# DLRM tower on Trainium2: two of three holds on the gather queue moved and one taken away, four transposes moved down TensorE's order

## The chip, the cores and the metric

One Trainium2 chip, one core. The metric is device time in microseconds (us) of one execution. TensorE (PE) computes matrix products and transposes, its weight loads are shown apart as PEld; ScalarE (ACT) and VectorE (DVE) copy and compute element by element; GpSimd (POOL) issues the gathers here; SyncE (SP) issues the other loads.

## The reference

For 512 samples, 26 embedding rows of 128 numbers are looked up, one from each table. With the dense row they make 27 vectors, and all products of two different ones are features of a three-layer network:

```python
sd = jnp.einsum('bfd,bd->bf', sparse_values, dense_features)
ss = jnp.einsum('bfd,bgd->bfg', sparse_values, sparse_values)
z = jnp.concatenate([dense_features, sd, ss[:, iu, ju]], axis=1)   # pairs f < g
h = jnp.concatenate([z, r_dense_features], axis=1)
h = jnp.maximum(h @ W_top1 + b_top1, 0.0)      # 607 -> 512
h = jnp.maximum(h @ W_top2 + b_top2, 0.0)      # 512 -> 256
y = h @ W_top3                                 # 256 -> 1
```

## The kernel before, in words

The samples are four tiles of 128. Twelve of the smaller tables are looked up on TensorE, for all samples at once: a table is split into a high and a low part and both are multiplied by a one-hot matrix (`table` steps, L485; the second halves of the last two tables are the `L498` instructions). The other 14 tables are gathered by POOL: one indirect DMA fetches 128 rows of one table for one tile, 56 gathers in all, k = 14 t + n for tile t and table n. Those rows lie one sample to a partition, so TensorE transposes them (`batch` steps, L520), up to four tables at a time, and ACT or DVE copies the result from PSUM into `embT` (`PLACERS` says who: ACT for batch 3.2, DVE for 3.0, 3.1 and 3.3).

Each tile t then goes through: `dots` D (128 matmuls, L540), `copies` C.0 and C.1 (16 copies on ACT, L314, and 16 on DVE, L387, from `dots` to `pairs`), `dense` P (L556), `layer1` L (L567), `relu1` R (ACT, L366), `layer2` M (L584), `relu2` H (ACT L370, DVE L428), `layer3` Y (L591) and `result` V (DVE, L432). `dots` is one set of PSUM banks: D of a tile waits until both engines have copied all of the tile before, and until all four batches of its own tile are placed.

The order is written by hand in `STEPS`: a word is a step, B3.0 is batch 0 of tile 3, and each of PE, ACT and DVE takes its own share of the steps in this order. So a step that is moved moves on every engine that has a part in it. Batches have 4, 4, 4 and 2 tables. B3.0, B3.1 and B3.2 are all transposed into the PSUM bank `turned`, so each waits until the one before it has been placed; B3.3 goes into a bank of `dots` and waits for C2.1.

POOL has its own loop (L274) and no steps. Gathers 7 to 42 wait for a count of finished tables, the first of each batch of tiles 2 and 3 waits until its buffer's older rows have been transposed, and `HELD_BY_DOTS` names gathers that also wait for a D:

```python
if k in HELD_BY_DOTS:
    pool.wait_ge(dots_done, HELD_BY_DOTS[k])
```

Before, gather 37 waits for D0, 44 for D1 and 51 for D2. B2.2 needs gathers 36 to 39, B2.3 needs 40 and 41, B3.0 needs 42 to 45, B3.1 46 to 49, B3.2 50 to 53, B3.3 54 and 55.

Of the kernel before, what the change touches and what calls it, by code (L numbers as in the profile page):

```python
# [53 lines left out]
def dlrm_tower(nc, gather_ids, onehot_ids, spread, tables, dense_t, w_pairs, w_dense, small, w2, identity,  # L54
# [9 lines left out]
    GATHERS_AHEAD, GATHERS_PER_TABLE = 4, 3  # L64

    LATER_GATHERS = GATHERS_AHEAD + GATHERS_PER_TABLE * (N_ONEHOT + 1)
    HELD_BY_DOTS = {37: 1, 44: 2, 51: 3}
    PAUSED_TABLES = (4, 6, 8)
    WARMING = 29
    WARMING_BETWEEN = 6  # L70
# [4 lines left out]
    with ctx:  # L75
# [108 lines left out]
        def loads_of(i):  # L184
# [5 lines left out]
        STEPS = [(NAMES[w[0]], *map(int, w[1:].split("."))) for w in """  # L190
            T0 T1 B0.0 T2 T3 B0.1 T4 B0.2 T5 B0.3 T6 B1.0 T7 B1.1 T8 T9 B1.2 T10.0 B1.3 T11.0 B2.0 T10.1
            D0 C0.0 T10.2 T10.3 T10.4 A10 T11.1 T11.2 T11.3 T11.4 C0.1 P0 B2.1 A11
            D1 C1.0 B2.2 B2.3 L0.0 L0.1 R0.0 R0.1 C1.1 P1 B3.0 M0 H0
            D2 Y0 C2.0 V0 B3.1 L1.0 L1.1 R1.0 R1.1 C2.1 P2 B3.2 M1 H1 B3.3 L2.0 R2.0
            D3 Y1 C3.0 V1 L2.1 R2.1 C3.1 P3 M2 H2
            L3.0 R3.0 Y2 V2 L3.1 R3.1 M3 H3 Y3 V3""".split()]

# [60 lines left out]
        def _(pool):  # L258
# [4 lines left out]
            for t in range(TILES):  # L263
                for n in range(N_GATHERED):
# [3 lines left out]
                    if GATHERS_AHEAD + GATHERS_PER_TABLE <= k < LATER_GATHERS:  # L268
                        pool.wait_ge(table_selected, (k - GATHERS_AHEAD) // GATHERS_PER_TABLE)
                    if k in HELD_BY_DOTS:  # L270
                        pool.wait_ge(dots_done, HELD_BY_DOTS[k])
                    if t >= 2 and n % BATCH_T == 0:
# [395 lines left out]
```

## Time and profile before

| what | us |
|---|---|
| median of 3 runs (lowest, highest) | 110.64 (110.51, 111.36) |
| the profiled execution's own time | 110.51 |
| its span from first to last instruction | 108.6 |
| PE busy | 104.1 (96%) |
| DVE busy | 75.6 (70%) |
| ACT busy | 66.1 (61%) |
| POOL busy | 60.4 (56%) |

The granted TensorE clock is full (1.00) over the whole span. The profiled execution is the lowest of the three, 1.9 us longer than its span and 0.13 under the median.

### The profile page before, as it was taken

What the parts mean: (1) busy time and instruction counts of PE and PEld (TensorE: products, weight loads), DVE (VectorE), ACT (ScalarE), POOL (GpSimd) and SP (SyncE); (2) the same over time, 40 slices, a digit from 0 to 9 for tenths busy, and PEclk for the clock granted to TensorE, in tenths of its full rate; (3) what the DMA queues carried; (4) which work ended last, traced back from release to release, by engine and by line L of the source; (5) the groups of instructions that cost most, each with busy time, mean ns of one, the idle gap of its engine ahead of it and who ended that gap; (6) DMA issues with size and microseconds to landing.
All of it is one profiled execution on the core that took longest, in us unless ns stands there. A gap on an engine that the chain in (4) does not pass through costs nothing.

```text
span 108.6 us, 2787 instructions
## 1 busy us (share of the span) xinstructions
PE 104.1 (96%) x1095; PEld 92.9 (86%) x1095; DVE 75.6 (70%) x204; ACT 66.1 (61%) x134; POOL 60.4 (56%) x62
## 2 busy tenths in 40 slices
PE   6999999999999999999899989999999999998992
PEld 6865888888888888888699979999999999998991
DVE  2199999999999999999950880599339830287001
ACT  5555528978997999989450993529133671286120
POOL 7877877877777777777700577777537600000000
PEclk9999999999999999999999999999999999999999
DMA  2899999784999999821200022212201110000000
GB/s 67 220 257 219 247 217 247 178 239 74 312 306 293 281 330 290 223 62 50 48 24 9 21 51 54 56 50 54 63 9 48 48 30 0 6 0 0 0 6 1
DMA packets 5199, 12.75 MB, mean 117 GB/s; under 512 B 1833, under 2 KB 1961, under 8 KB 5186
## 3 DMA queue, kind: packets, MB, share of 16 engines
q1 hardware_dynamic: 3346, 8.83, 30.4%
q0 software_dynamic: 1792, 3.67, 13.2%
q8 instruction: 9, 0.15, 0.6%
q10 hardware_dynamic: 48, 0.07, 0.2%
q14 instruction: 4, 0.03, 0.1%
HBM read 12.56 MB, written 0.00 MB: 116 GB/s over the span
## 4 chain that ended last, share of the span: by engine, by line
PE 39%; DVE 33%; DMA 14%; issue 6%; SPq 3%; ACT 2%; DVEq 0%
DVE onehot L394 16%; PE dots L540 14%; DMA table<-tbl 14%; PE hidden L567 10%; DVE low L402 9%; DVE pairs L387 9%; PE hidden L584 2%; PE last_layers L584 2%; ACT high L330 2%; SPq L226 2%; PE turned L520 2%; PE turned L567 2%; PE hidden L556 2%; PE hidden L485 1%; PE last_layers L591 1%
## 5 line engine op out<-in xcount | busy, mean ns | idle before, releaser
L274 POOL DMA_INDIRECT rows<-tbl,gather_idx x56 | 57.5, 1027 | 25.6 <-issue 14.8
L394 DVE TENSOR_SCALAR onehot<-ids_h 125x512 fp32r<-125x512 f16 x98 | 35.9, 425 | 3.3 <-ACT ids_h L320 3.3
L387 DVE COPY pairs<-dots 31x128 f32<-31x128 f32 (+5 forms) x64 | 18.4, 287 | 18.3 <-PE dots L540 16.5
L314 ACT COPY pairs<-dots 31x128 f32<-31x128 f32 (+5 forms) x64 | 16.1, 252 | 14.8 <-PE dots L540 13.5
L485 PE MATMUL dots<-onehot,high 125*128 125x512 f32 (+1 forms) x66 | 24.8, 395 | 0.1
L485 PE MATMUL dots<-onehot,low 125*128 125x512 f32 (+1 forms) x66 | 23.8, 380 | 0.1
L330 ACT CAST high<-table 125x1024 fp32r<-125x1024 f32 (+2 forms) x13 | 13.1, 1004 | 8.8 <-DMA table<-tbl 8.7
L402 DVE TENSOR_TENSOR low<-table,high 125x512 fp32r<-125x512 f32 (+1 forms) x24 | 16.6, 691 | 0.4 <-ACT high L330 0.3
L540 PE MATMUL dots<-embT 128*64 128x54 f32 x512 | 15.8, 223 | 0.4 <-DVE pairs L387 0.4
L540 PEld LDWEIGHTS dots<-embT 128*64 128x64 f32 x512 | 15.3, 138 | 1.0 <-issue 0.6
L485 PEld LDWEIGHTS dots<-onehot,low 125*128 125x128 f32 x66 | 12.3, 188 | 2.9 <-DVE low L402 0.8
L485 PEld LDWEIGHTS dots<-onehot,high 125*128 125x128 f32 x66 | 12.3, 188 | 2.6 <-ACT high L330 0.3
L567 PE MATMUL hidden<-pairs,wp 128*128 128x128 f32 x112 | 13.5, 276 | 0.3 <-DVE pairs L387 0.3
L567 PEld LDWEIGHTS hidden<-pairs,wp 128*128 128x128 f32 x112 | 12.9, 192 | 0.5 <-ACT pairs L314 0.5
L485 PE MATMUL hidden<-onehot,high 125*128 125x512 f32 (+1 forms) x32 | 12.6, 398 | 0.0
L485 PE MATMUL hidden<-onehot,low 125*128 125x512 f32 (+1 forms) x32 | 11.7, 369 | 0.5 <-DVE low L402 0.3
L347 ACT COPY embT<-dots 128x512 f32<-128x512 f32 (+1 forms) x8 | 8.6, 1080 | 0.0
L320 ACT CAST ids_h<-dots 125x512 f16<-125x512 f32 x12 | 7.5, 628 | 0.9 <-PE dots L458 0.9
L314 ACT COPY embT<-turned 128x512 f32<-128x512 f32 x7 | 7.9, 1124 | 0.0
L366 ACT ACTIVATE h<-hidden 128x256 f32<-128x256 f32 x7 | 2.5, 382 | 8.5 <-PE hidden L567 8.5
L485 PEld LDWEIGHTS hidden<-onehot,low 125*128 125x128 f32 x32 | 6.0, 188 | 1.8 <-DVE low L402 0.9
L485 PEld LDWEIGHTS hidden<-onehot,high 125*128 125x128 f32 x32 | 6.0, 188 | 1.3 <-DVE onehot L394 0.2
(55 smaller groups left out, 108.0 us busy)
## 6 DMA issues: line engine op xcount, KB each, us to landing
table<-tbl SPq DMA_DIRECT2D x10, 448.0 KB
wp<-w_pairs SPq DMA_DIRECT2D x2, 512.0 KB, 5.4
rows<-tbl,gather_idx POOLq DMA_INDIRECT x56, 4.3
table<-tbl SPq DMA_DIRECT2D x1, 560.0 KB
table<-tbl SPq DMA_DIRECT2D x10, 52.0 KB
wd<-w_dense SPq DMA_DIRECT2D x1, 512.0 KB, 4.7
w2s<-w SPq DMA_DIRECT2D x1, 512.0 KB, 5.2
table<-tbl SPq DMA_DIRECT2D x2, 224.0 KB
```

Source lines behind the costliest of these rows:

```text
L274: pool.indirect_dma_start(out=rows[:, t % 2, n, :], out_offset=None, in_=tables[GATHERED_TABLES[n]][:, :], in_offset=bass.IndirectOffsetOn ...
L314: return nc.scalar.copy(dst, src)
L320: nc.scalar.copy(ids_h[:, i % ID_BUFFERS, :], relative[i % 2][0:ROW_PARTS, :]).then_inc(ids_relative, 1)
L330: nc.scalar.copy(high[i % STAGES][:, first:last, :], table[i % TABLE_BUFFERS][:, first:last, :]).then_inc(high_ready, 1)
L347: nc.scalar.copy(embT[:, samples, TABLE_SLOT[t]], selected[t % STAGES][:, samples]).then_inc(table_placed, 1)
L387: return nc.vector.tensor_copy(dst, src)
L394: nc.vector.tensor_scalar(onehot[i % STAGES][:, c, :], ids_h[:, i % ID_BUFFERS, :], float(c), None, ALU.is_equal).then_inc(onehot_ready, 1)
L402: nc.vector.tensor_tensor(low[i % STAGES][:, first:last, :], table[i % TABLE_BUFFERS][:, first:last, :], high[i % STAGES][:, first:last, : ...
L485: last = nc.tensor.matmul(selected[t % STAGES][:, samples], part[t % STAGES][:, c, :], onehot[t % STAGES][:, c, samples], start=(part is h ...
L540: last = nc.tensor.matmul(dots[64 * h:64 * (h + 1), g, 0:2 * SLOTS], embT[:, s:s + 2, :].rearrange("p u s -> p (u s)"), embT[:, s:s + 2, 0 ...
L567: last = nc.tensor.matmul(hidden_block(t, m), wp[:, c, cols(m)], pairs[:, t % 2, c, :], start=False, stop=(c == PAIR_CHUNKS - 1), skip_gro ...
L584: last = nc.tensor.matmul(results[m], w2s[:, c, 128 * m:128 * (m + 1)], h1[:, t % 2, c, :], start=(c == 0), stop=(c == CHUNKS1 - 1))
```

## The change

The table of holds has two entries in place of three: gather 38 waits for D0 and gather 42 for D1, no gather waits for D2. In the order of steps B3.0 moves from before M0 to after V0, where B3.1 stood; B3.1 moves to where B3.2 stood; B3.2 moves behind M1 and H1, directly ahead of B3.3.

```diff
-    HELD_BY_DOTS = {37: 1, 44: 2, 51: 3}
+    HELD_BY_DOTS = {38: 1, 42: 2}
...
-            D1 C1.0 B2.2 B2.3 L0.0 L0.1 R0.0 R0.1 C1.1 P1 B3.0 M0 H0
-            D2 Y0 C2.0 V0 B3.1 L1.0 L1.1 R1.0 R1.1 C2.1 P2 B3.2 M1 H1 B3.3 L2.0 R2.0
+            D1 C1.0 B2.2 B2.3 L0.0 L0.1 R0.0 R0.1 C1.1 P1 M0 H0
+            D2 Y0 C2.0 V0 B3.0 L1.0 L1.1 R1.0 R1.1 C2.1 P2 B3.1 M1 H1 B3.2 B3.3 L2.0 R2.0
```

On TensorE, between L0 (above the first row) and L2.0 (last row); the transposes are the L520 rows, and the two stretches around D2 and L1 that stay as they are lie between the two pieces:

```order
@@ -248,5 +248,4 @@
 L567 MATMUL hidden<-pairs,wp 128x128 x16
 L556 MATMUL hidden<-denseT,wd 128x128 x4
-L520 MATMUL turned<-ident,rows 128x128 x4
 L584 MATMUL last_layers<-h,w2s 128x128 x4
 L584 MATMUL hidden<-h,w2s 128x128 x4
@@ -259,4 +258,5 @@
 L584 MATMUL last_layers<-h,w2s 128x128 x4
 L584 MATMUL hidden<-h,w2s 128x128 x4
+L520 MATMUL turned<-ident,rows 128x128 x4
 L520 MATMUL dots<-ident,rows 128x128 x2
 L567 MATMUL hidden<-pairs,wp 128x128 x8
```

Four transposes stand one fewer ahead of D2, and one batch more behind M1, ahead of D3. The number of instructions between D1 and D3 is the same.

On DVE, the copies C1.1 and C2.1 (19x4x32 rows) with what follows them:

```order
@@ -72,5 +72,4 @@
 L387 COPY pairs<-dots 7x4x32 x2
 L387 COPY pairs<-dots 19x4x32 x2
-L387 COPY embT<-turned 128x4x128
 L428 TENSOR_SCALAR h<-hidden,smalls 128x128
 L387 COPY pairs<-dots 31x4x32
@@ -84,4 +83,5 @@
 L387 COPY pairs<-dots 7x4x32 x2
 L387 COPY pairs<-dots 19x4x32 x2
+L387 COPY embT<-turned 128x4x128
 L428 TENSOR_SCALAR h<-hidden,smalls 128x128
 L387 COPY embT<-dots 128x2x128
```

The placing of B3.0 no longer stands behind C1.1; the placing of B3.1 now stands behind C2.1 and ahead of DVE's half of H1. On ACT the placing of B3.2 and its half of H1 change places.

On POOL, of the change, gathers 36 to 46, with their waits:

```order
L274 DMA rows<-tbl,gather_idx 128x128 [waits transposed,table_selected]
L274 DMA rows<-tbl,gather_idx 128x128 [waits table_selected]
L274 DMA rows<-tbl,gather_idx 128x128 [waits dots_done,table_selected]
L274 DMA rows<-tbl,gather_idx 128x128 [waits table_selected]
L274 DMA rows<-tbl,gather_idx 128x128 [waits transposed,table_selected]
L274 DMA rows<-tbl,gather_idx 128x128 [waits table_selected]
L274 DMA rows<-tbl,gather_idx 128x128 [waits transposed,dots_done,table_selected]
L274 DMA rows<-tbl,gather_idx 128x128 x3
L274 DMA rows<-tbl,gather_idx 128x128 [waits transposed]
```

Gather 37 has lost its wait for a D, 38 and 42 have one; 42 has three waits, and behind it only the waits for free buffers are left.

## Rows read from the trace of the kernel before

**Rows 1.** The chain of waits, in order of time: start us, length us, what.

```profile
55.89 3.90 PE dots L540 x128
...
64.58 0.30 DVE pairs L387
...
65.02 3.94 PE dots L540 x128
...
73.35 0.89 PE hidden L556 x8
74.24 0.44 PE turned L520 x4
74.68 0.89 PE last_layers L584 x8
75.57 0.89 PE hidden L584 x8
76.46 3.87 PE dots L540 x128
...
90.38 3.90 PE dots L540 x128
94.28 0.02 issue
94.30 0.28 DVE pairs L387
```

**Rows 2.** The timeline of ACT: start us, length us, instruction, [idle before <-releaser].

```profile
73.38 0.66 ACT L366 ACTIVATE h<-hidden 128x256 f32<-128x256 f32 x2 [2.17 <-PE hidden L567]
73.93 2.14 ACT L314 COPY pairs<-dots 14x96 f32<-14x96 f32 x8
```

**Rows 3.** The timeline of weight loads (PEld), D1 to D3.

```profile
64.99 3.84 PEld L540 LDWEIGHTS dots<-embT 128*64 128x64 f32 x128 [0.58 <-issue]
...
76.39 3.81 PEld L540 LDWEIGHTS dots<-embT 128*64 128x64 f32 x128
...
84.67 0.97 PEld L556 LDWEIGHTS hidden<-denseT,wd 128*128 128x128 f32 x8
85.75 0.42 PEld L520 LDWEIGHTS turned<-ident,rows 128*128 128x128 f32 x4
86.13 0.97 PEld L584 LDWEIGHTS last_layers<-h,w2s 128*128 128x128 f32 x8
87.02 0.97 PEld L584 LDWEIGHTS hidden<-h,w2s 128*128 128x128 f32 x8
88.15 0.20 PEld L520 LDWEIGHTS dots<-ident,rows 128*128 128x128 f32 x2 [0.15 <-DMA rows<-tbl,gather_idx]
88.32 1.87 PEld L567 LDWEIGHTS hidden<-pairs,wp 128*128 128x128 f32 x16
```

**Rows 4.** The timeline of POOL around the three holds.

```profile
53.20 0.97 POOL L274 DMA_INDIRECT rows<-tbl,gather_idx  x1 [0.30 <-issue]
60.55 0.94 POOL L274 DMA_INDIRECT rows<-tbl,gather_idx  x1 [6.38 <-PE dots L540]
...
80.62 0.94 POOL L274 DMA_INDIRECT rows<-tbl,gather_idx  x1 [2.88 <-PE dots L540]
...
85.61 0.95 POOL L274 DMA_INDIRECT rows<-tbl,gather_idx  x1 [0.30 <-issue]
```

**Rows 5.** Gathers by issue, median us to landing: first 76.5 to 77 us, then 85 to 86.

```profile
rows<-tbl,gather_idx POOLq DMA_INDIRECT x1, 4.3
...
rows<-tbl,gather_idx POOLq DMA_INDIRECT x2, 2.6
```

**Rows 6.** Windows with D1, D2, D3, line L540 alone: PE, PEld busy, clock, DMA share, GB/s.

```profile
65.00:69.00 4.00, 3.94 (x128) 3.84 (x128) 1.00 0.23 55
76.40:80.30 3.90, 3.90 (x128) 3.81 (x128) 1.00 0.16 38
90.30:94.30 4.00, 3.94 (x128) 3.81 (x128) 1.00 0.02 4
```

**Rows 7.** The timeline of DVE around C2.1.

```profile
83.04 1.04 DVE L387 COPY embT<-turned 128x512 f32<-128x512 f32 x1
84.11 2.49 DVE L387 COPY pairs<-dots 14x96 f32<-14x96 f32 x8
```

## The prediction

> **What bounds the kernel now.** I read the page first: PE is busy for 96% of the span at full clock, so what counts is whether PE gets more or less to do, or stands still. The chain of waits says where it does not stand still [rows 1]: from the start of D1 at 65.02 to the end of D3 at 94.28 every piece of the chain is PE, one behind the other. Ahead of it, D0 runs from 55.89 to 59.79 and D1 waits for DVE's last copy of C0, which ends at 64.88. Behind D3 the chain goes over to DVE's copies and then to tile 3's layers, which the change leaves alone. So the change is worth what it does to the start of D3, now at 90.38 in the chain, 90.31 by the weight loads. I work in the frame of the weight loads (PEld), since their starts are recorded where they wait.
>
> **Part 1, the gathers around D0 and D1.** Gather 37 is no longer held. Gather 36 starts at 53.20 and takes 0.97, and one gather follows another after 0.30 [rows 4], so 37 starts at 54.47 and ends before 55.5, while PE is busy with tables. It was not late before, so nothing is gained. From D0's end on, the row of gathers is one ahead: 38 starts at 60.55, where 37 did. Then 41 ends some 4 x 1.25 later, at 65.2, and 42 waits for D1. B2.2 and B2.3, which come right after D1, get gathers 38 to 41 1.25 us earlier than now; no wait before them stands in the chain, so this too is worth 0.
>
> What could be gained is quiet beside the dots. D0 has no gather beside it already before the change: POOL stands idle for 6.38 us until 60.55 [rows 4]. D1 loses its gathers. But D1 with gathers beside it and DMA at 23% is busy for 3.94 us, and D3 with DMA at 2% for the same 3.94 [rows 6]. In the chain they take 3.94 and 3.90 [rows 1]. So quiet is worth 0 to 0.04 us, and D2, which has one gather beside it now (3.87) and will have three, can pay the same back. I take 0.
>
> **Part 2, B3.0 leaves its place ahead of M0.** Four transposes are 0.44 us in the chain [rows 1]. D2's loads would start at 76.39 - 0.44 = 75.95. But D2 waits for all copies of C1.1, and ACT's end at 73.93 + 2.14 = 76.07 [rows 2]. ACT cannot begin earlier: its two relus wait for the end of L0. From the last copy to the loads of a D there are 0.11 us (64.88 to 64.99, D1) [rows 1, 3]. So D2 starts at 76.18: 0.21 of the 0.44 is gained, and a new stall of 0.23 stands where the transposes were. Those transposes filled time in which PE would have waited anyway. M0 itself does not stall: its first operand is ready after one relu of about 0.38 and its second at 73.38 + 0.66 = 74.04, and M0's third matmul comes about 0.24 after 73.97.
>
> **Part 3, the same four transposes come back ahead of D3.** Between D2 and D3 there are now four batches in place of three. Everything from D2 on is 0.21 earlier, until the loads of P2 end at 84.67 + 0.97 - 0.21 = 85.43 [rows 3]. B3.1 there takes 0.44, to 85.87. (Before, B3.2 stood there and started 0.11 late, at 85.75: gather 53 issued at 85.61 - 2 x 1.25 = 83.11 had only just landed. B3.1's gathers are in long before, so this 0.11 goes.) M1 takes what lies between its first load and the end of its last, 87.99 - 86.13 = 1.86, to 87.73. B3.2 takes 0.44, to 88.17. Then B3.3 is ready to go, if gathers 54 and 55 are in.
>
> **Part 4, when the last gather lands.** Gather 42 now waits for D1 and all later ones stand behind it on POOL. D1 ends at 65.02 + 3.94 = 68.96. How fast POOL resumes is seen twice: 0.76 after the end of D0 (59.79 to 60.55), and 0.29 after the end of D2 (76.46 + 3.87 = 80.33 to 80.62) [rows 1, 4]. So gather 42 starts at 69.25 to 69.72. From there 13 gathers at (85.61 - 80.62) / 4 = 1.25 [rows 4] bring gather 55 to 85.47 to 85.97, about where it is now (85.61), since the hold behind D2 is gone and the queue never stops. The last gather took from 85.61 to 88.15 to release PE [rows 3, 4], 2.54 us, and by the view of DMA issues 2.6 [rows 5]. So it lands at 88.0 to 88.5, against PE's 88.17: no wait, or up to 0.34. B3.3 took 0.17 from its first load to that of L2.0 (88.15 to 88.32), so L2.0 starts at 88.34 to 88.68, where it started at 88.32.
>
> The Trainium skill (DMA: Bandwidth & Descriptors, section Anatomy of one DMA, SWDGE path) prices such a transfer at about 2.0 us fixed plus bytes over 436 GB/s. For 64 KB that is 2.15 us, an estimate from that page; by it gather 55 would land at 88.12 at the latest, PE would not wait, and the sum would be at its lower end. The row says 2.54, and I go by the row.
>
> **The queues behind.** DVE has a tight spot. Shifted by 0.21, it ends C2.0 and V0, places B3.0 to 83.87 and does C2.1, 2.49 us, to 86.39 [rows 7]. Only then does it place B3.1, 1.04 us, to 87.47. B3.2 uses the same bank `turned` and waits for this: 87.47 + 0.11 = 87.58 against 87.73 for PE. It holds by 0.15. ACT places B3.2 from about 88.3 to 89.4, and D3 wants it at 90.3. B3.3 is placed by DVE in about 0.6, also in time. B3.0 needs gather 45, issued near 73.4, for transposes at about 80.4, and B3.1 gather 49, near 78.4, for 85.4: covers of 7 us each. B3.2 needs gather 53, issued at 83.0 to 83.5, by 87.7, a cover of at least 4.2.
>
> **The sum.** D3's loads start at 90.31 + 0.02 to 90.31 + 0.36, and the rest of the program is as before. Between two ends so near each other, each with one row behind it, I take the middle, +0.2. The profiled execution's 110.51 becomes 110.7; it lies 0.13 under the median of its runs, 110.64, from which the forecast is 110.8. In words: 0.44 goes, 0.23 is paid back at once as a stall, 0.44 comes back later, 0.11 to 0.26 of waiting for gathers goes, and may come again at B3.3.
>
> **The rivals.** A measurement of this kernel can tell about 1% (1.1 us) from no change.
>
> *Quiet pays, or the waits go entirely.* If gather 42 starts at 69.25, D1 gains its 0.04, and the copies of ACT beside D1's end also run a little quicker without gathers, then the stall at D2 shrinks by some 0.2 and no gather is waited for: 110.64 + 0.02 - 0.04 - 0.2 = 110.4. Against it: the rows of D1 and D3 show no such cost. To be faster by over 1% it would have to take more than a quarter out of a D, and nothing in rows 6 leaves room for that.
>
> *The last gathers land late, slower than before.* One gather, issued at 76.80 beside D2, took 4.3 us to land, not 2.6 [rows 5]. If 54 or 55 did so, it would land at 89.8 to 90.3, and B3.3, which now stands directly behind B3.2, and all of L2.0 and D3 behind it would wait 1.6 to 2.1: 112.3 to 112.8. It decides from a landing of 2.2 to 2.7 us on, and costs 1% from about 3.4 on. For it: in the changed kernel the queue runs without a break from D1 on, so a late one has no slack behind it. Against it: the last gathers of the row had 2.6, and DMA is nearly idle there.
>
> *DVE's placing of B3.1 becomes the wait.* If C2.1 or the copies ahead of it on DVE are 0.5 later than I work out, B3.2 waits 0.35 and L2.0, D3 with it: about 111.1. The margin of 0.15 is thin, but DVE's copies of this kind vary little.
>
> *The change does not do what it says.* The holds might not bind, if POOL reached gathers 38 and 42 only after D0 and D1. Gather 37 ends at 55.5, long before 59.79, and 41 at 65.2, before 68.96, so both bind.
>
> **How the numbers follow.** Forecast of next to no change, 0.2 up: chance 0.66, its own range 110.4 to 111.2 (ends +0.02 and +0.36, and some 0.2 to each side for the spread of medians, which the three runs, 110.51 to 111.36, suggest). Quiet pays: 0.16, near 110.4. DVE's placing: 0.10, near 111.1. Late landing: 0.06, near 112.5. Something else that I do not see, on either side: 0.02. The range of 110.2 to 111.6 takes in the first three and leaves out the fourth. Faster by over 1%: 0.04, since only the unknown can do it with a part of the second case; slower by over 1%: 0.08, the late landing and part of the unknown and of DVE's case; within 1%: 0.88.
>
> **What would show it.** Right: D2's loads at about 76.2, with a wait of about 0.2 for ACT's copies ahead of them; D1 and D2 of unchanged length; POOL idle from about 65.2 to 69.3 or 69.7 and not again; the last gather at 85.5 to 86.0; D3's loads at 90.3 to 90.7; a wait for a gather ahead of B3.3 of 0 to 0.35. Wrong: D1 or the copies beside it shorter by more than 0.2; a wait for DVE ahead of B3.2; a gather that takes over 3 us to land; or any shift ahead of 65.02, where nothing should move.

## The result, and the profile after

| | before | after |
|---|---|---|
| median us, 20 runs each, same chip | 110.72 | 111.44 |
| lowest and highest | 110.17, 112.37 | 110.75, 112.25 |
| ratio after / before, 95% interval | | 1.0067 (1.0042 to 1.0092) |
| profiled execution | 110.51 | 111.28 |
| its span | 108.6 | 109.4 |

The change is slower by 0.7%, about 0.7 us. That is inside the forecast range of 110.2 to 111.6 and within 1%, but it is clear of noise, more than the forecast 0.2, and above the 110.4 to 111.2 that the likeliest case had for itself. Medians here and below are over all executions, ratios over the fast ones, since a few executions fall into a slower state. The chain of waits of the changed kernel, in order of time, near its end (start us, length us, what):

```profile
80.80 0.94 POOL rows L274
81.74 0.30 issue
82.04 0.94 POOL rows L274
82.99 0.30 issue
83.29 0.95 POOL rows L274
84.24 0.30 issue
84.54 0.94 POOL rows L274
85.49 0.30 issue
85.79 3.10 DMA rows<-tbl,gather_idx
88.89 0.04 issue
88.93 0.44 PE dots L520 x2
89.37 1.79 PE hidden L567 x16
91.16 3.90 PE dots L540 x128
```

Before, this stretch of the chain was PE alone [rows 1]. Now it runs back from the two transposes of B3.3 to the landing of gather 55, and from there along POOL's row of gathers, one every 1.25 us, to the one that waited for D1. In the timeline of weight loads the wait has its length (the last row is cut off by the end of the view):

```profile
64.83 3.84 PEld L540 LDWEIGHTS dots<-embT 128*64 128x64 f32 x128 [0.59 <-issue]
...
76.11 3.84 PEld L540 LDWEIGHTS dots<-embT 128*64 128x64 f32 x128 [0.45 <-issue]
...
87.53 0.47 PEld L520 LDWEIGHTS turned<-ident,rows 128*128 128x128 f32 x4
88.93 0.20 PEld L520 LDWEIGHTS dots<-ident,rows 128*128 128x128 f32 x2 [0.93 <-DMA rows<-tbl,gather_idx]
...
91.08 1.01 PEld L540 LDWEIGHTS dots<-embT 128*64 128x64 f32 x32
```

B3.3 waits 0.93 where it waited 0.15 [rows 3]. This execution reaches D1 0.16 earlier than the one of before (64.83 against 64.99), which has nothing to do with the change: later profiles of the same two kernels reach it at 65.07 and 65.30. So I compare the stretch from D1's loads to D3's: 91.08 - 64.83 = 26.25, against 90.31 - 64.99 = 25.32. That is +0.93, and what lies outside the stretch gives 0.16 of it back.

POOL, ACT and DVE in the changed kernel, each from its own timeline:

```profile
54.31 1.36 POOL L274 DMA_INDIRECT rows<-tbl,gather_idx  x1 [0.30 <-issue]
60.38 0.94 POOL L274 DMA_INDIRECT rows<-tbl,gather_idx  x1 [4.72 <-PE dots L540]
...
69.56 0.94 POOL L274 DMA_INDIRECT rows<-tbl,gather_idx  x1 [4.49 <-issue]
...
85.79 0.94 POOL L274 DMA_INDIRECT rows<-tbl,gather_idx  x1 [0.30 <-issue]
```

```profile
73.76 2.13 ACT L314 COPY pairs<-dots 14x96 f32<-14x96 f32 x8
```

```profile
83.85 2.48 DVE L387 COPY pairs<-dots 14x96 f32<-14x96 f32 x8
86.36 1.05 DVE L387 COPY embT<-turned 128x512 f32<-128x512 f32 x1
```

Both holds bind: POOL is idle before gather 38 and before gather 42. ACT's copies end at 75.89 and D2's loads start at 76.11. DVE places B3.1 by 87.41, just before PE wants the bank at 87.53.

And the windows with D1 and D2 of line L540 alone (columns as in [rows 6]):

```profile
64.80:68.80 4.00, 3.94 (x128) 3.84 (x128) 1.00 0.08 23
76.10:80.10 4.00, 3.94 (x128) 3.84 (x128) 1.00 0.23 60
```

D1 without gathers beside it takes 3.94 us, as it did with them.

### The profile page after: what moved, and what is told of

Its sections match the earlier page's. It is cut to its first block, busy times and chain, and to the rows that moved or that the text cites. A ratio compares the mean times of both kernels' runs of the same rounds, so it can differ in the third digit from the quotient of the medians.

```text
span 109.4 us, 2787 instructions
## 1 busy us (share of the span) xinstructions
PE 104.0 (95%) x1095; PEld 92.8 (85%) x1095; DVE 75.7 (69%) x204; ACT 66.0 (60%) x134; POOL 60.6 (55%) x62
## 4 chain that ended last, share of the span: by engine, by line
DVE 35%; PE 20%; issue 14%; DMA 13%; POOL 11%; ACT 3%; POOLq 1%; SPq 1%; DVEq 0%; ACTq 0%
DVE onehot L394 18%; POOL rows L274 11%; DMA table<-tbl 10%; DVE low L402 8%; DVE pairs L387 8%; PE dots L540 7%; PE hidden L567 3%; PE last_layers L464 3%; DMA rows<-tbl,gather_idx 3%; PE turned L567 2%; PE hidden L485 1%; ACT high L330 1%; POOLq L75 1%; ACT embT L347 1%; ACT ids_h L320 1%
## 5 line engine op out<-in xcount | busy, mean ns | idle before, releaser
L540 PEld LDWEIGHTS dots<-embT 128*64 128x64 f32 x512 | 15.3, 138 | 1.3 <-issue 1.0
L540 PE MATMUL dots<-embT 128*64 128x54 f32 x512 | 15.8, 223 | 0.7 <-DVE pairs L387 0.4
```

Of the source, the lines that this page charges most:

```text
L540: last = nc.tensor.matmul(dots[64 * h:64 * (h + 1), g, 0:2 * SLOTS], embT[:, s:s + 2, :].rearrange("p u s -> p (u s)"), embT[:, s:s + 2, 0 ...
```

## The experiments

A job is one session on one chip, and only times of one job can be compared directly; the kernel before ran beside each job at 110.82 to 110.88 us. In the first job the changed kernel ran again with each half of the change and with one hold moved by one gather; in the second, holds were taken away; in the third, TensorE's stream of instructions was made shorter. "Landing" is the time from the start of a gather's instruction on POOL to the weight loads that it releases.

**The changed kernel again**, no edit.

> The changed kernel once more, for a second profile and for a time beside the next ones. Theory (the last gather is what costs): B3.3 waits again for gather 55, and what it waits follows from how long that gather takes to land: 88.17 is when PE is ready (frame of the first profile), gather 55 starts at about 85.9, so a landing of 2.5 us gives a wait of 0.3, one of 3.1 a wait of 0.9. About 111.4 us, ratio 1.005 to 1.009. Rival (the stall ahead of D2 and the longer queue on DVE cost it): the time is the same, but it would be 111.4 also in an execution whose last gather lands in 2.5.

111.35 us, ratio 1.0032 (1.0000 to 1.0064), less than the 1.005 that I expected at least, though the interval reaches it. Gather 55 starts at 86.06 and releases B3.3 3.17 us later:

```profile
89.23 0.20 PEld L520 LDWEIGHTS dots<-ident,rows 128*128 128x128 f32 x2 [0.98 <-DMA rows<-tbl,gather_idx]
```

The slow landing was no accident of one execution: 3.17 with a wait of 0.98, as the expectation had it for a landing of 3.1.

**The new order alone.**

```diff
-    HELD_BY_DOTS = {38: 1, 42: 2}
+    HELD_BY_DOTS = {37: 1, 44: 2, 51: 3}
```

> The new order of steps with the old holds (37, 44, 51). Theory (the last gather costs): the hold behind D2 ends 0.2 us earlier than before since D2 does, so gather 55 starts 0.2 earlier, at 85.4, while B3.3 comes when it did in the changed kernel, at 88.2; it waits 0 to 0.3. About 110.7 to 110.9, ratio 1.000 to 1.002. Rival (the stall ahead of D2 or DVE's queue costs it): all of the loss is in the order, so 111.4, ratio 1.006.

111.10 us, ratio 1.0001 (0.9973 to 1.0030). D1 to D3 takes 25.74 with a wait of 0.40 for gather 55, which took 3.06 (85.76 to 88.82). The wait is smaller since the gather starts earlier against PE. The ratio is the expected one, and its interval leaves out the rival's 1.006, but allows some tenths of a us either way.

**The new holds alone**, with the old order of steps.

```diff
-    HELD_BY_DOTS = {37: 1, 44: 2, 51: 3}
+    HELD_BY_DOTS = {38: 1, 42: 2}
```

> The new holds (38, 42) with the old order of steps. Theory (quiet beside D1 is worth nothing, a late gather is): B3.0 stands ahead of M0 at 73.97, but gather 45 starts at 69.7 + 3 x 1.25 = 73.5 and lands at 76.0; PE waits 2.0 us there and nothing gives it back. About 112.7, ratio 1.018. Rival (quiet beside the first two dots is worth something): the wait is there, but D1 or the copies next to it are shorter, so clearly under 112.5, with D1's 128 matmuls under 3.94 us.

112.39 us, ratio 1.0111 (1.0070 to 1.0153).

```profile
76.06 0.42 PEld L520 LDWEIGHTS turned<-ident,rows 128*128 128x128 f32 x4 [1.99 <-DMA rows<-tbl,gather_idx]
```

The wait of 2.0 ahead of B3.0 came as computed, and D1 has its usual length. Gather 45, which it waits for, started at 73.51 and landed in 2.55. The time did not come as computed: I expected 1.018, which is outside the interval, and had written that nothing gives the wait back. D1 to D3 takes 27.02, 1.7 over the first profile of before, and not 2.0: everything behind is late enough that neither B3.2 nor B3.3 waits for a gather. By the ratio the distance is smaller still, 1.2 us, as it must be if the kernel before has a longer wait in some of its executions (below). So the new order is what makes the new holds bearable, but it does not make them useful.

**One gather more ahead of the hold.**

```diff
-    HELD_BY_DOTS = {38: 1, 42: 2}
+    HELD_BY_DOTS = {38: 1, 43: 2}
```

> The changed kernel, but gather 43 waits for D1 in place of 42, so one gather more runs ahead of D1's end, and the waiting one has one wait in place of three. Theory (the last gather costs): POOL resumes at 0.3 to 0.76 after D1 with gather 43, so gather 55 starts at 84.2 to 84.7, 1.25 to 1.7 earlier, and lands by 87.8 at the latest: no wait ahead of B3.3. The wait of 0.3 to 0.9 goes: about 110.7, ratio 1.000. Rival (the loss is in the stall ahead of D2 or on DVE): stays at 111.4. Second question: if the wait's form sets the 0.76 us of POOL's return, it is about 0.3 here.

110.66 us, ratio 0.9966 (0.9936 to 0.9996), 0.7 us under the changed kernel beside it. The timeline of POOL at the hold, and of weight loads at B3.3:

```profile
69.12 0.94 POOL L274 DMA_INDIRECT rows<-tbl,gather_idx  x1 [2.75 <-PE dots L540]
...
84.09 0.94 POOL L274 DMA_INDIRECT rows<-tbl,gather_idx  x1 [0.30 <-issue]
```

```profile
88.25 0.25 PEld L520 LDWEIGHTS dots<-ident,rows 128*128 128x128 f32 x2
```

No wait is left at B3.3, with the same order and the same stall ahead of D2. This shows that the last gather is what cost, not DVE's queue. (D1 to D3 still takes 25.58, with 0.22 of it in a gap behind D1 for which the profile gives no releaser.) Gather 43 waits for D1 alone and starts 0.27 after its end (64.91 + 3.94 = 68.85 to 69.12); gather 42, with three waits, starts 0.76 after it.

**The kernel before again**, no edit.

> The kernel before once more, for a second profile. In its first profile an instruction fetch of 16 KB starts at 88.6 us, behind the last gather's landing (2.54 us after its start); in all four profiles with the new order of steps it starts at 86.4 to 86.9, and where the last gather starts at about 86 it takes 3.0 to 3.2 us. Theory (the fetch holds up one DMA engine, and its time varies from one execution to the next): here the fetch may fall at 86.5 too, and then gather 55 lands in about 3.0 and B3.3 waits 0.5 to 0.6 in place of 0.15, with a time near 111.0. Rival (the new order moves the fetch): it stays at 88.6 and the landing at 2.5. The ratio is 1.000 either way.

110.92 us, ratio 0.9983 (0.9942 to 1.0023). Its profile shows what the first one did not:

```profile
89.35 0.20 PEld L520 LDWEIGHTS dots<-ident,rows 128*128 128x128 f32 x2 [1.17 <-DMA rows<-tbl,gather_idx]
```

Gather 55 started at 85.93 and took 3.42, with the instruction fetch (the DMA that brings an engine its next instructions, described below) at 87.0 to 87.5; D1 to D3 took 26.21. I had expected a landing of about 3.0 and a wait of 0.5 to 0.6. So the kernel before has this wait too in some of its executions, and my first profile was one that missed it. It is not the new order that puts the fetch there.

**Without the hold behind D2**, in the kernel before.

```diff
-    HELD_BY_DOTS = {37: 1, 44: 2, 51: 3}
+    HELD_BY_DOTS = {37: 1, 44: 2}
```

> The kernel before without the hold of gather 51 behind D2; the other two holds and the order stay. Gathers 51 to 55 start from 78.05 on, 2.57 us earlier. Theory (late gathers are what costs, quiet beside D2 is worth nothing): the waits ahead of B3.2 and B3.3 (0.11 and 0.15, more where the landing is slow) go, D2 keeps its 3.87 to 3.90 us, about 110.4 to 110.5, ratio 0.995 to 0.998. Rival (quiet beside a D or the copies is worth something): 1.000 or above.

110.39 us, ratio 0.9979 (0.9944 to 1.0015). No wait for a gather; D1 to D3 25.15, of which 0.21 is a gap behind D1 that the profile gives no releaser for. The size is as expected, but the interval reaches over 1: in time alone this run decides nothing.

**Without the hold behind D1**, in the changed kernel.

```diff
-    HELD_BY_DOTS = {38: 1, 42: 2}
+    HELD_BY_DOTS = {38: 1}
```

> The changed kernel without the hold of gather 42 behind D1; only 38 waits, for D0. Gather 55 starts at about 81.8, four us earlier. Theory (quiet is worth nothing): as the run with gather 43 held, no wait ahead of B3.3, ratio 0.996 to 0.998, D1's 128 matmuls at 3.94 us with gathers beside them. Rival (quiet beside D1 is worth something): slower than that run by over 0.2%, with D1 over 3.94.

110.76 us, ratio 1.0011 (0.9972 to 1.0050). I had expected 0.996 to 0.998, so the time does not bear the expectation out, and against the run with gather 43 held, which belongs to another job, it is unclear. The windows are clear: D1 with gathers all along it, DMA at 19%, is as long as without, and D1 to D3 takes 25.36, no gather waited for.

```profile
64.90:68.90 4.00, 3.94 (x128) 3.84 (x128) 1.00 0.19 57
```

**No hold at all**, in the kernel before, twice.

```diff
-    HELD_BY_DOTS = {37: 1, 44: 2, 51: 3}
+    HELD_BY_DOTS = {}
```

> The kernel before with no hold at all: gathers 37 to 40 run beside D0, and the last one starts at about 77.5. Theory (quiet is worth nothing beside any D): as the run without the hold behind D2, ratio 0.995 to 0.998, D0 at 3.90 us in the chain. Rival (quiet beside D0 is what the holds are for): D0 or the copies C0 behind it are longer and D1 starts later than 65.0; then ratio 1.000 or more.

> The kernel before with no hold at all, once more for its time, as the candidate that beats both: no stall ahead of D2 as with the new order, no wait for any gather. From D1 to D3 it took 25.00 us, against 25.32 and 26.2 in the two profiles of the kernel before. If that is what counts, ratio 0.994 to 0.998. Rival (the gathers beside D0 and the copies C0 cost it what it gains): 0.999 or above.

110.17 us, ratio 0.9979 (0.9938 to 1.0019), and 110.03 us, ratio 0.9946 (0.9917 to 0.9974). Both profiles have 25.00 from D1 to D3. The windows of the first with D0 and D1:

```profile
55.80:59.80 4.00, 3.94 (x128) 3.81 (x128) 1.00 0.20 55
65.00:69.00 4.00, 3.94 (x128) 3.84 (x128) 1.00 0.20 53
```

and the same window of the kernel before, where D0 has nothing beside it:

```profile
55.80:59.80 4.00, 3.94 (x128) 3.81 (x128) 1.00 0.03 6
```

D0 is as long with 20% of DMA beside it as with 3%, and DVE's 16 copies of C0 take 5.06 against 5.07. So neither D0 nor DVE's copies of C0 gain by the hold. This version is faster than the kernel before, in the second run beyond its interval (by 0.5%, 0.3% to 0.8%); it never ran in one job with the changed kernel, but that one's ratio to the kernel before was above 1 in both of its jobs.

**Nine warming matmuls in place of 29**, in the changed kernel and in the kernel before.

```diff
-    WARMING = 29
+    WARMING = 9
```

> The changed kernel with 9 warming matmuls at the start in place of 29, which takes some 40 instructions (a load and a matmul each) out of TensorE's stream ahead of the place. Theory (a 16 KB fetch of TensorE's instructions takes one DMA engine for about 1 us just when gathers 54 and 55 use it, and the fetch follows the count of instructions): the fetch near 86.5 comes some 40 instructions later, behind M1, at 88 or after; gather 55 lands in 2.4 to 2.6 us, and the wait ahead of B3.3 falls from 0.9 or 1.0 to 0.3 or 0.4. About 0.5 us faster, unless the start suffers. Rival (gathers late in the row are slow for a reason of their own, as two in flight at once or the transposes beside them): the fetch moves, landing stays at 3.0 or more.

> The kernel before with 9 warming matmuls in place of 29. Theory: the fetch moves behind gather 55's landing here too, so it lands in 2.4 to 2.6 as in the first profile (not in 3.4 as in the second), with a wait ahead of B3.3 of 0.1 to 0.2, and 110.4 to 110.6 us. Then what is left between this and the changed kernel with 9 is the later return of POOL and the stall ahead of D2: 0.3 to 0.5 us. Rival: landings scatter between 2.5 and 3.4 as before, independent of the fetch.

110.67 us, ratio 0.9991 (0.9950 to 1.0031), and 110.65 us, ratio 0.9989 (0.9953 to 1.0026). The fetch did move: it starts between 89.0 and 89.5 in the first, between 90.0 and 90.5 in the second. The same gather, from 85.84 and from 85.58, then releases B3.3 after 2.51 us in both, after a wait of 0.29 as expected in the first and of 0.27, more than the expected 0.1 to 0.2, in the second:

```profile
88.35 0.20 PEld L520 LDWEIGHTS dots<-ident,rows 128*128 128x128 f32 x2 [0.29 <-DMA rows<-tbl,gather_idx]
```

```profile
88.09 0.20 PEld L520 LDWEIGHTS dots<-ident,rows 128*128 128x128 f32 x2 [0.27 <-DMA rows<-tbl,gather_idx]
```

A cause that is not in the gathers, in POOL or in the order of steps was moved, and the landing went from 3.1 to 2.5. The changed kernel's ratio to the kernel before fell from 1.0032 to 0.9991, about 0.5 us, where D1 to D3 lost 0.6 to 0.7; but that is across two jobs, and the two intervals overlap.

All profiles in one table, in us. "Landing" is that of gather 55, where B3.3 waited for it; "fetch" is the window of 0.5 us in which the 16 KB instruction fetch starts:

| kernel | D1 to D3 | gather 55 | landing | wait at B3.3 | fetch |
|---|---|---|---|---|---|
| before | 25.32 | 85.61 | 2.54 | 0.15 | 88.5 |
| before, again | 26.21 | 85.93 | 3.42 | 1.17 | 87.0 |
| before, 9 warming | 25.29 | 85.58 | 2.51 | 0.27 | 90.0 |
| before, no hold at D2 | 25.15 | 83.14 | | none | 86.5 |
| before, no hold | 25.00 | 77.39 | | none | 86.0 |
| before, no hold, again | 25.00 | 77.25 | | none | 86.0 |
| new holds alone | 27.02 | 85.99 | | none | 88.0 |
| after | 26.25 | 85.79 | 3.14 | 0.93 | 86.5 |
| after, again | 26.32 | 86.06 | 3.17 | 0.98 | 86.0 |
| after, 9 warming | 25.62 | 85.84 | 2.51 | 0.29 | 89.0 |
| new order alone | 25.74 | 85.76 | 3.06 | 0.40 | 86.5 |
| after, 43 held | 25.58 | 84.09 | | none | 86.5 |
| after, no hold at D1 | 25.36 | 81.70 | | none | 86.0 |

Every landing of over 3 us has a fetch that starts at 86.0 to 87.5, and every one of 2.5 has it at 88.5 or later. The fetch in the views of DMA after (86.5 to 87.0) and before (88.5 to 89.0), as queue, kind: packets, MB, share of 16 engines:

```profile
q8 instruction: 1, 0.02, 11.6%
...
q8 instruction: 1, 0.02, 15.4%
```

The packet records show the meeting itself. In the first profile of after the fetch runs from 86.85 to 87.78; 15 of gather 55's 16 packets of 4 KB start between 87.44 and 87.67, and the last one at 87.80, 0.02 after the fetch ends. In the second profile of before and in the run with the new order alone the last packet starts 0.02 before the recorded end of the fetch (88.19 against 88.21, 87.65 against 87.67). In the second profile of after the fetch (86.47 to 87.88) holds back a packet of gather 54 (87.86 to 88.30), behind which gather 55's last one follows at 88.30. The records do not name the engine of a packet; that the late one stood behind the fetch on one engine is read from these times.

## Why the prediction was right, and which term was too small

*The time:* inside the range, but partly by luck. The range was drawn to take in quiet (near 110.4) and DVE's placing (near 111.1) as well, and neither is what came: the likeliest case alone ended at 111.2. Of the signs of being wrong that I had listed, one came: a gather that takes over 3 us to land. D3's loads at 91.08 and the wait of 0.93 lie outside the 90.3 to 90.7 and the 0 to 0.35 that were to show it right.

*What bounds the kernel, and the sign:* right. PE sets the end from D1 to D3, nothing ahead of D1 changed beyond the scatter of executions, and the loss is at the one place where part 4 put a possible wait, B3.3.

*Part 1, quiet is worth nothing:* right, shown for D1 (3.94 with and without) and for D0 by the runs without holds. Gather 37 took 1.36 and not 0.97; it ran beside DVE's sum of weights, but whether that made it longer was not tested, and nobody waits for it.

*Part 2, the stall ahead of D2:* right in kind, a little short. D2 was to gain 0.21; from D1's loads to D2's it gained 11.40 - 11.28 = 0.12. From ACT's last copy to the loads there are 0.22 (75.89 to 76.11), where I had taken 0.11 from D1, behind a copy of DVE. The cost of the order without any wait for gathers can be read off: 25.36 - 25.00 = 0.36, where the forecast's stall was 0.23.

*Part 3, the row of steps behind D2:* right to 0.10. From D2's loads to PE's being ready for B3.3 the forecast had 88.17 - 76.18 = 11.99, and it took 88.00 - 76.11 = 11.89. This 0.10 makes good the 0.09 that part 2 was short, so that PE was ready at the forecast distance from D1's loads (23.18 and 23.17), which is luck to that extent. The waits of before did go, and were worth a little more than my 0.11 to 0.26: 25.32 - 25.00 = 0.32.

*Part 4, the last gather:* the term that was too small: a wait of 0 to 0.34 was forecast, and it was 0.93. Its start was forecast between 85.47 and 85.97; it is 85.79, or 85.95 with the 0.16, at the upper end. I took the middle between a return of POOL after 0.76 and one after 0.29. The rows gave a reason to choose, since the gather that came back after 0.29 had one wait and the one after 0.76 had more; gather 42 has three. The larger error is the landing, 2.54 by rows 3 and 5, but 3.14. With the sum redone, +0.36 for the stall, -0.32 for the waits of before, +0.89 for the wait now (26.25 - 25.36) is +0.93, what the two profiles show.

*Which part of that is the change's?* With the fetch out of the way in both kernels, the stretch is 25.62 against 25.29: +0.33, next to the upper end of the forecast (+0.36). With the fetch on the gather in both, it is 26.32 against 26.21: +0.11. Only the first pair of profiles, with the fetch on one side alone, shows 0.93. The medians lie between: +0.7 and +0.5 us in two jobs. This fits a kernel before which escapes the fetch in some executions and a changed one which does so less often. How often either does is not known, since each run has one profiled execution; that share stays open. Single times do not tell it either: with no hold at all no profile shows a wait for a gather, and yet 15 of the 24 executions took 109.74 to 110.22 us and the other nine 110.49 to 111.54. What makes those longer is open. The time of the two kernels with 9 warming matmuls against each other stays open too: their ratios are alike within intervals of 0.4%, and a difference of 0.3 us could hide there.

*The rivals:* "quiet pays" fell with every window. "The last gathers land late" named the place and the sign, but priced a landing of 4.3, and I gave it 0.06; what came is 3.1, a smaller case of it. I had not looked for the cause, and the trace of before had it: the gather that took 4.3 [rows 5] meets the fetch before this one. 15 of its packets of 4 KB start by 78.84, the fetch runs from 79.09 to 80.03, and the last packet starts at 80.01. My argument that DMA is nearly idle there did not touch this, since one fetch is enough. DVE's placing of B3.1 came within 0.12 of mattering (87.41 against 87.53) and did not.

## What to carry to other kernels

None of the three holds bought anything here. Before you pay for quiet, look whether the work beside the gathers is longer with them than without: compare one stage in both. When a queue ends only just ahead of its last reader, one median landing is no price: leave it a us (the landings here went from 2.51 to 3.42), or start the queue earlier. And a stage that is moved out of a stall frees nothing, since the stall stays where the stage was.

## What the hardware showed that I had not expected

An instruction fetch (one packet of 16 KB, 0.9 to 1.4 us in the DMA records of these profiles) makes a small gather late when they meet: 3.06 to 3.42 us to release its reader, against 2.51 to 2.54 without. In the first profile of after the fetch took 0.93, one of the last gather's packets of 4 KB then 0.48, and a single completion packet of 4 bytes came 0.38 behind all the others (88.27 against 87.89). PE's loads start another 0.66 later, where they start 0.37 after the last completion packet of an undisturbed landing (87.78 to 88.15, first profile of before). So the late packet accounts for 0.38 of the longer landing directly; what the other 0.3 is, the records do not show. The Trainium skill (DMA: Bandwidth & Descriptors) says in its section Queues, rings and completion order that each DMA engine goes round its queues a whole packet at a time, and in its section Why a DMA increments its semaphore by 16 and not by 1 that all data has landed only when the full 16 increments are in; the late packet, right behind the fetch, agrees with this. The Trainium skill's fit for such a transfer (DMA: Bandwidth & Descriptors, section Anatomy of one DMA, SWDGE path), 2.0 us fixed plus bytes over 436 GB/s, gives 2.15 us for 64 KB, an estimate; no gather whose landing could be read at a wait here met it, the quickest taking 2.51.

The moment of the fetch follows the count of TensorE's instructions, and is not fixed by it alone. With some 40 fewer at the start of the program it came at 89.4 and 90.2, in one profile each, and eight fetches of 16 KB were left of nine. With the full count it came at 86.3 to 87.1 in nine of the eleven profiles, at 88.7 in the first of before, and at 88.5 with the new holds alone, where all work behind B3.0 is late. What sets it within one program stays open.

POOL comes back from a wait for a D after 0.27 to 0.29 us where the gather has one wait (43, 51), and after 0.76 to 0.79 where it has two or three (37, 38 and 42). That the number of waits is the reason is not shown: in the first case POOL had been idle for 2.75 to 2.88 us, in the second for 4.49 or more, and no run separates the two.
